# Second attention of a three-stage decoder layer: packing the two end tiles of the queries by head

## The reference

```python
q_hk  = (hidden_q @ Wq.T).reshape(B, S, H, K)             # H = 16 heads, K = 128
q_big = einsum('bshk,hkq->bshq', q_hk, w_kc_q)            # 192 features a head
q_big = q_big * cos + rotate_half(q_big) * sin            # features 0..95 and 96..191 are the two halves
q_r   = einsum('bshq,hqr->bhsr', q_big, W_qr)             # 64 a head
k_r   = einsum('bld,hdr->bhlr', kv_r, W_kr)
scores = einsum('bhsr,bhlr->bhsl', q_r, k_r); attn = softmax(scores)
```

## Time and profile before

| what | value |
|---|---|
| median of 3 runs | 1347.61 us (1345.91 to 1348.05) |
| span of the profiled execution, first to last instruction | 1343.3 us |
| its own time as a run | the page gives the span alone; the median of the runs is 4.3 us above the span |
| PE busy | 1269.2 us (94%) |
| DVE busy | 843.1 us (63%) |
| ACT busy | 715.6 us (53%) |
| POOL busy | 470.9 us (35%) |
| contraction L716 on PE | 62.3 us, 512 records |
| takes L1174 on DVE | 192 operations, mean 686 ns |

### The profile page before, as it was taken

The page is one execution under the profiler, slowest core; times in us unless marked ns, Lnnn a source line. Parts: engine busy times, 40 slices in busy tenths (PEclk is TensorE's granted clock), DMA queues, the critical chain, the costliest instruction groups (busy, mean ns, idle before and its releaser), DMA issues.

```text
span 1343.3 us, 27486 instructions
## 1 busy us (share of the span) xinstructions
PE 1269.2 (94%) x9712; PEld 989.2 (74%) x9712; DVE 843.1 (63%) x1986; ACT 715.6 (53%) x2746; POOL 470.9 (35%) x467
## 2 busy tenths in 40 slices
PE   5799999999999788999999999989899999999998
PEld 4578888888887565666666666557788888888887
DVE  6788888888888676666656656765453333433333
ACT  2788888889887553444444444465232332423322
POOL 3122113112212134544544534541053353533532
PEclk9999999999999899999999999999999999999999
DMA  6011001100102101002002001000325342254230
GB/s 221 16 25 49 18 17 25 49 17 17 31 19 92 35 1 76 1 1 76 1 1 75 1 1 60 1 1 1 107 58 142 74 120 56 39 137 78 56 93 31
DMA packets 29810, 64.54 MB, mean 48 GB/s; under 512 B 6912, under 2 KB 12160, under 8 KB 28416
## 3 DMA queue, kind: packets, MB, share of 16 engines
q1 hardware_dynamic: 29696, 63.05, 17.6%
HBM read 52.42 MB, written 2.23 MB: 41 GB/s over the span
## 4 chain that ended last, share of the span: by engine, by line
PE 74%; DVE 10%; ACT 7%; issue 4%; POOL 2%; DMA 2%; SPq 1%; DVEq 0%; POOLq 0%; ACTq 0%
PE ps L531 31%; PE ps L923 9%; PE ps L647 5%; PE ps L716 4%; PE ps L679 4%; PE ps L820 4%; ACT ea L1434 3%; PE ps L810 3%; PE ps L792 3%; PE ps L800 2%; PE ps L670 2%; PE ps L586 2%; DMA cw<-comb_d 2%; ACT ea L1478 1%; DVE xnt L991 1%
## 5 line engine op out<-in xcount | busy, mean ns | idle before, releaser
L1798 POOL TENSOR_TENSOR sg<-sg,cw 128x512 f32<-128x512 f32 x88 | 113.5, 1290 | 260.1 <-ACT sg L1597 253.1
L1375 DVE TENSOR_TENSOR hh<-ps,sg 128x512 f32<-128x512 f32 x100 | 69.2, 692 | 178.6 <-POOL sg L1798 162.0
L1401 ACT ACTIVATE hhh<-hh 128x512 fp32r<-128x512 f32 x100 | 63.2, 632 | 214.7 <-DVE hh L1375 214.7
L1401 ACT ACTIVATE pt<-ps 128x512 f32<-128x512 f32 x128 | 76.9, 600 | 179.3 <-PE ps L800 122.6
L1434 ACT ACTIVATE ea<-ps,negmax 128x64 f32<-128x64 f32 (+1 forms) x512 | 164.6, 341 | 6.0 <-DVE negmax L1127 6.0
L531 PE MATMUL ps<-xnh,wch 128*128 128x512 f32 x400 | 157.0, 393 | 0.7 <-ACT pt L1401 0.7
L1174 DVE TENSOR_TENSOR qcs<-ps,tabb 128x512 f32<-128x512 f32 x192 | 123.6, 686 | 53.4 <-PE ps L531 53.1
L531 PE MATMUL ps<-xnl,wch 128*128 128x512 f32 x400 | 156.9, 392 | 0.0
L531 PE MATMUL ps<-xnh,wcl 128*128 128x512 f32 x400 | 155.6, 389 | 0.0
L1665 POOL TENSOR_TENSOR ea<-ea,rden 128x128 f32<-128x128 f32 (+1 forms) x128 | 62.1, 506 | 256.2 <-DVE rden L1083 256.2
L1672 POOL TENSOR_TENSOR eb<-eb,rsum 128x512 f32<-128x512 f32 x64 | 66.9, 1045 | 160.3 <-DVE rsum L1218 160.3
(11 more groups left out here) (153 smaller groups left out, 3349.6 us busy)
## 6 DMA issues: line engine op xcount, KB each, us to landing
raw_w<-in_rawb_dram SPq DMA_DIRECT2D x4, 2432.0 KB, 9.0
kva<-ktmp SPq DMA_DIRECT2D x64, 128.0 KB, 2.4
cw<-comb_d SPq DMA_DIRECT2D x32, 256.0 KB, 5.0
raw_w<-in_rawc_dram SPq DMA_DIRECT2D x4, 1920.0 KB, 8.0
cw<-comb_d SPq DMA_DIRECT2D x16, 224.0 KB, 4.3
raw_a<-in_wqk_dram SPq DMA_DIRECT2D x4, 768.0 KB, 5.4
cw<-comb_d SPq DMA_DIRECT2D x16, 192.0 KB, 6.0
cw<-comb_d SPq DMA_DIRECT2D x16, 160.0 KB, 5.5
```

The costliest lines, as they stand in the source:

```text
L1375: dve.tensor_tensor(hh[:, par, :], bank(C_U[par]), sg[:, par, :], ALU.mult).then_inc(c_h, 1)
L1401: return act.activation(dst, src, ACT.Copy)
L1798: pool.tensor_tensor(sg[:, par, :], sg[:, par, :], cw[:, c % 2, t, :], ALU.mult).then_inc(c_hs, 1)
```

## The change

Tile 4 now holds the last 32 features of both halves of heads 0 and 1 (rows: head 0 first half, head 0 second half, head 1 first half, head 1 second half), and tile 5 those of heads 3 and 2. So each head has its 64 rows in one tile. Four things follow:

- The contraction has 3 steps: `(4, 5)` first, then `(0, 2)` and `(1, 3)`. The first stands alone in slot 1 of the unit j = 3, the other two in the item `("qr", 0)`.
- Matching rows of a sine product now lie in the same tile 32 rows apart. DVE takes such a tile with one cosine product of 128 rows and four sine products of 32 rows, each written 32 rows up or down.
- POOL adds both tiles in one operation of 2x512 elements (`tails`), in the unit j = 1.
- The tiles come in the order 4, 5, 0, 1, 2, 3, and tile 4 waits for the weights of head 1 only. Tile 5, now in slot 1 of unit 12, waits for head 3, prepared in slot 0 of unit 12. The tables are loaded in 12 transfers and not 16.

Everything behind line 178 stands one or more lines lower in the changed kernel: L1174 is L1182 and L1186, L716 is L724, L1206 is L1219, L1212 is L1225, L1218 is L1231, L1088 is L1096, L1177 is L1190.

```diff
+        B_ORDER = [4, 5, 0, 1, 2, 3]
-        B_STEP = {(t // 2, t % 2): [("qb", t)] for t in range(XT)}
+        B_STEP = {(i // 2, i % 2): [("qb", t)] for i, t in enumerate(B_ORDER)}
...
         def b_segments(t):
-            late = 96 * (t % 2)
             if t >= 4:
-                return [(h, late + 64, 32, 32 * i) for i, h in enumerate((0, 3, 1, 2))]
-            return [(h, late, 64, 64 * i) for i, h in enumerate((0, 1) if t < 2 else (3, 2))]
+                return [(h, 96 * j + 64, 32, 64 * i + 32 * j) for i, h in enumerate((0, 1) if t == 4 else (3, 2))
+                        for j in range(2)]
+            return [(h, 96 * (t % 2), 64, 64 * i) for i, h in enumerate((0, 1) if t < 2 else (3, 2))]
...
             def b_contract(g_to, c, n, steps):
-                pe.wait_ge(b_rp, XT // 2 * q + (2 if steps[0] == 0 else 3))
+                pe.wait_ge(b_rp, XT // 2 * q + (1 if steps[0] == 0 else 3))
...
-                    t01, t32 = ((0, 2), (1, 3), (4, 4), (5, 5))[k]
+                    t01, t32 = ((4, 5), (0, 2), (1, 3))[k]
                     for h, at, t in ((0, 0, t01), (1, 64, t01), (3, 0, t32), (2, 64, t32)):
                         d = slice(64 * (h % 2), 64 * (h % 2) + 64)
-                        last = pe.matmul(pairs[h // 2][d, :], mq[at:at + 64, t, d], qcs[at:at + 64, t, 0, :],
-                                         start=k == 0, stop=k == 3, skip_group_check=True)
+                        last = pe.matmul(pairs[h // 2][d, :], mq[at:at + 64, t, d], qcs[at:at + 64, b_at(t), 0, :],
+                                         start=k == 0, stop=k == 2, skip_group_check=True)
...
             def prep_of(g_to, t):
-                head = 1 if t < 2 else HG - 1
+                head = 1 if t in (0, 1, 4) else HG - 1
...
                 if kind == "qb":
-                    for m in range(2):
-                        last = dve.tensor_tensor(quads(qcs[:, t, m, :]), quads(bk), bcast(tabb[:, b_table(t), m, :]),
+                    for m in range(2 if t < 4 else 1):
+                        last = dve.tensor_tensor(quads(qcs[:, b_at(t), m, :]), quads(bk), bcast(tabb[:, b_table(t), m, :]),
+                                                 ALU.mult)
+                    for at in range(0, 128 if t >= 4 else 0, 32):
+                        to = at + 32 if at % 64 == 0 else at - 32
+                        last = dve.tensor_tensor(quads(qcs[to:to + 32, b_at(t), 1, :]), quads(bk)[at:at + 32],
+                                                 tabb[at:at + 32, 2, 1, :].unsqueeze(1).broadcast_to([32, CB, S]),
                                                  ALU.mult)
...
+            def tails(done):
+
+                pool.wait_ge(b_if, done + 1)
+                pool.tensor_tensor(qcs[:, 0:2, 0, :], qcs[:, 0:2, 0, :], qcs[:, 0:2, 1, :], ALU.add).then_inc(b_rp, 1)
...
+                if u % CB == 1:
+                    tails(b_item(g, u - 1, 1, ("qb", 5)))
                 for s in range(2):
                     for what in b_slot(u, s, final):
-                        if what[0] == "qb" and what[1] % 2:
+                        if what[0] == "qb" and what[1] in (1, 3):
                             rope(g + 1 if c == NC - 1 else g, (c + 1) % NC, what[1] // 2, b_item(g, u, s, what))
 
             for u in range(2):
                 a_unit(NG, u, drain=True)
-                rope(0, 0, u, XT + 2 * u + 1)
-
+
+            tails(XT + 1)
+            rope(0, 0, 0, XT + 3)
             ln_low(2 * NC - 2)
-            rope(0, 0, 2, XT + 5)
+            rope(0, 0, 1, XT + 5)
```

More of the change, by code:

```diff
@@ L177, in decoder_kernel @@
         kvin = sb(bm, "kvin", [128, B, XC])
-        tabb = sb(bm, "tabb", [128, 4, 2, S])
+        tabb = sb(bm, "tabb", [128, 3, 2, S])
+        sb(bm, "b_gap3", [128, 2 * S])
         kvt = sb(bm, "kvt", [128, B, XC])
@@ L319, in bcast, with b_at @@
             return tab.unsqueeze(1).broadcast_to([128, CB, S])
-        B_STEP = {(t // 2, t % 2): [("qb", t)] for t in range(XT)}
+        B_ORDER = [4, 5, 0, 1, 2, 3]
+        def b_at(t):
+            return B_ORDER.index(t)
+        B_STEP = {(i // 2, i % 2): [("qb", t)] for i, t in enumerate(B_ORDER)}
         B_STEP[CB - 1, 2] = [("qr", 0)]
@@ L327, in b_segments @@
         def b_segments(t):
-            late = 96 * (t % 2)
             if t >= 4:
-                return [(h, late + 64, 32, 32 * i) for i, h in enumerate((0, 3, 1, 2))]
-            return [(h, late, 64, 64 * i) for i, h in enumerate((0, 1) if t < 2 else (3, 2))]
+                return [(h, 96 * j + 64, 32, 64 * i + 32 * j) for i, h in enumerate((0, 1) if t == 4 else (3, 2))
+                        for j in range(2)]
+            return [(h, 96 * (t % 2), 64, 64 * i) for i, h in enumerate((0, 1) if t < 2 else (3, 2))]
         def b_rows(h):
             first = 0 if h < 2 else 2
-            return first, 64 * (h % 2 if h < 2 else 3 - h), 32 * (0, 3, 1, 2).index(h)
+            return first, 64 * (h % 2 if h < 2 else 3 - h)
         def b_split(ap, h):
-            first, wide, narrow = b_rows(h)
-            return [ap[:, first:first + 2, :, wide:wide + 64], ap[:, 4:6, :, narrow:narrow + 32]]
+            first, at = b_rows(h)
+            return [ap[:, first:first + 2, :, at:at + 64],
+                    ap[:, 4 + first // 2, :, at:at + 64].rearrange("p k (j a) -> p j k a", j=2)]
         def b_columns(bk):
@@ L349, in b_table @@
         def b_table(t):
-            return t % 2 + 2 * (t >= 4)
+            return 2 if t >= 4 else t % 2
         def b_slot(u, s, final=False):
@@ L371, in b_places @@
             return B_PLACES[isinstance(g, int) and g == NG - 1]
-        B_FIRST = [("prep", t) for t in range(XT)] + [("qb", t) for t in range(XT)] + [("qr", 0)]
+        B_FIRST = [("prep", t) for t in range(XT)] + [("qb", t) for t in B_ORDER] + [("qr", 0)]
         BF = len(B_FIRST)
@@ L468, in _ @@
                 sp.dma_start(tabb[at + 32:at + 64, 1, :, :], in_tabb[0:32, 1]).then_inc(b_ctx, 16)
-            for at in range(0, 128, 32):
                 sp.dma_start(tabb[at:at + 32, 2, :, :], in_tabb[64:96, 0]).then_inc(b_ctx, 16)
-                sp.dma_start(tabb[at:at + 32, 3, :, :], in_tabb[32:64, 1]).then_inc(b_ctx, 16)
+                sp.dma_start(tabb[at + 32:at + 64, 2, :, :], in_tabb[32:64, 1]).then_inc(b_ctx, 16)
             sp.wait_ge(s_cst2, 2)
@@ L610, in slot @@
                                 ln_ready(NC)
-                            b_do(0, 0, what, XT + what[1])
+                            b_do(0, 0, ("qb", B_ORDER[what[1]]), XT + what[1])
                             continue
@@ L728, in b_do @@
                 if kind == "qr":
-                    b_contract(g_to, c, n, (2, 3)).then_inc(b_it, 1)
+                    b_contract(g_to, c, n, (1, 2)).then_inc(b_it, 1)
                     return
@@ L775, in slot @@
                         place[0] = b_par(g, u, 2, ("qr", 0))
-                        b_contract(g + 1 if c == NC - 1 else g, (c + 1) % NC, b_item(g, u, 2, ("qr", 0)), (0, 1))
+                        b_contract(g + 1 if c == NC - 1 else g, (c + 1) % NC, b_item(g, u, 2, ("qr", 0)), (0,))
                     for what in b_slot(u, s, final):
@@ L899, in _ @@
                 if what[0] == "qr":
-                    b_contract(0, 0, item, (0, 1))
+                    b_contract(0, 0, item, (0,))
                 b_do(0, 0, what, item)
@@ L1038, in kv_step @@
                 if i == 0:
-                    dve.wait_ge(b_ctx, 16 * 16)
+                    dve.wait_ge(b_ctx, 16 * 12)
                     for d in (0, half):
@@ L1101, in slot @@
                         if what[0] == "qb":
-                            b_take(what, XT + what[1], (XT + what[1]) % 2, None)
+                            b_take(("qb", B_ORDER[what[1]]), XT + what[1], (XT + what[1]) % 2, None)
                 if two:
```

2 lines of the change are left out of this document (1 added, 1 removed).

## The result

| | before | changed |
|---|---|---|
| median (runs) | 1346.94 us (4, 1345.91 to 1348.05) | 1387.4 us (4, 1387.14 to 1388.43) |
| span of the profiled execution | 1343.3 us | 1385.3 us |
| mean granted clock of PE | 0.993 | 0.981 |

The ratio is 1.0303, with an interval of 1.0289 to 1.0318: 40.5 us slower. The forecast was 1375.0 us with a range to 1387, so the direction was right, and the loss was 13 us more than the sum gave (on the spans of the profiled executions 42.1 us and not 27.3).

What follows compares the result with a forecast made beforehand. PE was taken to bound stage B, with 0.84 us of room for DVE's takes. Ordinary chunks 13.2, preparation 9.8, drain 2.5 and unit 8 1.8 made +27.3 us on the 1343.3 us span: median 1375 us, range 1359 to 1387.

Steps and rivals of the forecast that it cites:

- The waits of an ordinary chunk: Stage B: PE waits 1.50 us for `obl`, then 0.4 in the next unit; net 1.2 us a chunk, 13.2 for 11.
- The wait for the weights: Preparation chunks: PE waits 2.6 us ahead of tile 5 for head 3's weights; these three chunks cost 9.8 us in all.
- The `xnt`: Drain and last group's unit 8: without POOL's addition beside it, `xnt` gives back 1.9 and 1.8 us.
- The price from the keys of stage A: Each operation of a take priced at 0.70 us, like stage A's 64-row key products: 3.50 us a take, not 1.21.
- Rival 2: DVE's pieces overlap like an ordinary take's products, 0.61 us each, 3.05 a take: 1361 us; chance 0.12.
- Rival 1: Stage B absorbs the DVE burst if a take fits into 2.05 us: 1333 us, faster; chance 0.06, including 0.02 for no difference.
- rival 3: More loss: `xnt` stays slow, PE falls to 1.2 GHz behind waits, or pieces cost up to 0.80: around 1383 us; chance 0.12.
- I count nothing there: Chunk made while stage A drains: PE waits for POOL's additions ahead of the last two contraction steps; priced at nothing.
- I price it alike: First ordinary chunk of stage B, with layer norm turns in place of `obl`: priced like the others, 1.2 us.
- Rival 4: Lone contraction step costs PE more than 0.94 us, or L810 waits for ACT's copy: up to 14 higher, 1389; chance 0.03.
- The second wait at the preparation: Unit 13's first tile waits 1.6 us more, until tile 5 is taken from the bank it writes.
- Unit 8 of the last group: DVE-bound there: two takes add 4.6 us, `xnt` gives back 1.8, the step saves 0.94: +1.8 us.

Runs made afterwards that it cites:

- experiment 7: The kernel before, with POOL's first pair of additions in stage A's drain moved behind its second normalisation: 1346.24 us, ratio 0.9996.
- experiment 1: The changed kernel with the shift by 32 rows left out, one sine product of 128 rows, so two operations a take: 1335.97 us, ratio 0.9922 to before.
- experiment 2: The changed kernel with five overlapping 128-row products a take of tiles 4 and 5 in stage B, no exchange there: 1370.14 us, ratio 1.0175 to before.
- experiment 8: The changed kernel with two sine pieces of 64 rows in place of four of 32, exchanging the wrong rows: 1347.37 us, ratio 1.0007 to before.
- experiment 3: The changed kernel with unread matmuls filling PE's long waits in the drain and at the preparations: 1380.65 us, ratio 1.0257 to before.
- experiment 10: The kernel that shifts rows by DMA, with POOL's `tails` moved ahead to the end of unit j = 1: 1336.37 us, ratio 0.992 to before.
- experiment 4: The changed kernel with tile order 0, 1, 2, 4, 3, 5 and POOL adding tiles 4 and 5 singly: 1401.55 us, ratio 1.0402 to before.
- experiment 9: The changed kernel with the row shift by four DMA transfers a chunk and `tails` in unit j = 2: 1341.37 us, ratio 0.9959 to before.
- experiment 6: The changed kernel with head 3's weights prepared one slot earlier, in slot 2 of unit 11: 1382.92 us, ratio 1.027 to before.

## Why the prediction was right, and where it failed

**Right, by its own steps.** The price of a piece: 0.69 long and 0.70 apart, a take 3.49 (forecast 3.50). The waits of an ordinary chunk: 1.57 and 0.41. The wait for the weights: 2.49. The `xnt`: 1.38 at both places, with POOL's addition beside it as the cause in the drain (experiment 7, which doesn't show by what means the two meet). The price from the keys of stage A was the step that decided the sign, and experiments 1 and 2 show that the pieces, by their number and their lack of overlap, are the whole loss. Rival 2 was out by 0.1 us an operation. Rival 1's point, 2.05 us a take, fits ordinary chunks: experiment 8 with 2.13 has nearly no wait there. Its total of 1333 doesn't follow from that point, since experiment 8 took 1347.

**The step that failed: the clock was left out of the sum.** The prediction priced each wait by its own length, with the work behind it at full speed. It had seen the 1.2 GHz level behind a poor stretch and put it into rival 3. The waits that it forecast itself, at the preparation (2.49 measured) and for the `xnt` in the drain (4.09), are followed by windows at 0.56 to 0.72 of full clock. So is a third, for which it said "I count nothing there": the wait for POOL's additions ahead of the last two steps grew from 1.81 to 2.67, with 0.50 in 515 to 519 us behind it. With the three filled (experiment 3) the drain and the preparation cost 2.6 and 10.8 in place of 4.0 and 12.8, and the first chunk 2.5 us less. Together that is 5.9 of the 14.8 us that the spans are apart from the sum; the medians of the runs differ by 6.7.

**Terms that were mis-sized.**
- "I price it alike": the first chunk of stage B. Even at full clock it costs 3.4 and not 1.2. Its waits are others: behind the one of 2.67, 1.01 for the take of tile 4's bank, 0.67 for the exponentials, six more of 0.2 to 0.5, together 3.8 against 0.7 before. That chunk starts right behind the drain, and most likely DVE had no spare time there to take up the burst; this is read from the trace, and was not tried by itself.
- The step left alone costs 1.02 and not 0.94, so the change saves 0.86 a chunk: 15 x 0.08 = 1.2 us. The two waits, 0.08 longer than forecast, make the rest of the 1.7 that the ten ordinary chunks are over their 12.0. Rival 4 had that mechanism, and most of its size came to nothing.
- The second wait at the preparation was 0.45 in group 1 and not 1.6, but other waits stood for it, and at full clock the sum nearly held (3.6 against 3.3).
- Unit 8 of the last group: +3.3 and not +1.8. PE's waits for `obl` are 2.52, 0.31 and, for the next `xnt`, 1.23; before, they were 0.19 and 1.31. That is 2.6 more, less the 0.86 saved: 1.7, the forecast. The rest is most likely the clock again, 0.84 and 0.73 in the 8 us behind the wait of 2.52 and 1.00 in 857 to 861 of the kernel before; no run filled that wait, so this is read and not shown.
- 1.3 us before the drain and 1.1 behind the last chunk lie outside the change. Other runs of this study move by as much or more there (2.2 and 1.4 in experiment 7).
- "Moves with it": the median was to stay 4.3 us above the span of the profiled execution, and is 2.1 above it in the changed kernel. So some 2 us of the miss don't show in the medians, by chance: 14.8 on the spans became 12.4.

The range ended at 1387, 0.4 us too low: it held the direct waits with their errors, and left little room for what a wait does to the work behind it. Rival 3 named that effect, with "a few us more", and stood outside the sum.

## What to carry to other kernels

- A DVE product of 512 columns lasted 0.69 us on 32 rows as on 128, and the pieces that were written to other rows came 0.70 apart, where products in place came 0.59 apart. Count operations and not elements, and see whether an idle DMA queue can move the rows: here four transfers a chunk cost nothing that could be measured, and turned a loss of 40 us into a gain of 11 (experiment 10).
- A long wait of PE should be priced with the granted clock behind it, from a row at either level. Here the waits of 2.3 to 4.1 us were mostly followed by a lower clock, which added 0.2 to 1.3 us each at the preparation, 1.4 in the drain and 2.5 in the first chunk; the wait of 1.57 in ordinary chunks left it at 1.00 (660 to 700 us). Look also at waits that a new order of the work lengthens.
- When a burst is moved or split, follow every queue behind it. Experiment 4 lost 29 us to POOL's order alone, and experiment 9 lost 5 us to one addition a unit too late.

## What the runs showed of the hardware that I had not expected

- Four transfers of 128 KB from SBUF to SBUF, between rows 32 apart, landed 2.3 us after their issue (median of 60), and the operations of PE, DVE and ACT beside them kept their length (DVE's products 686 ns in experiment 10 and 687 in experiment 1, ACT's exponentials 366 and 368).
- A group of four 64-row matmuls alone takes 1.02 us in the chain of waits, two groups in a row 1.88.
- Filling PE's waits with useless matmuls made a kernel faster (6.7 us here), though no wait became shorter by it.
- The same wait of 2.3 us, three times in one execution, was followed by a lower clock twice and by 1.00 once (experiment 6).
